# First expert layer of a two-layer transformer on one Trainium2 core: every expert on every row, or rows routed to their two experts

## The chip, the cores and the metric

The kernel runs on one core of one Trainium2 chip, in one launch. The metric is the device time in microseconds (us), the median of several executions. Engines are named as the profile names them: PE is TensorE, ACT ScalarE, DVE VectorE, POOL GpSimd, SP SyncE (it only issues DMAs here).

## The reference

4096 rows (4 sequences of 1024) of 128 numbers pass through attention, a mixture of experts, a second attention and a second mixture of experts, each behind a layer norm and added to x. The change touches the first mixture of experts:

```python
shared = new_gelu(xf @ Wfc_s + bfc_s) @ Wproj_s + bproj_s        # 128 -> 512 -> 128
probs = softmax(xf @ Wr)                                         # 8 experts
topk_p, topk_i = top_k(probs, 2)
topk_p = topk_p / sum(topk_p)
gate = zeros((N, 8)).at[arange(N)[:, None], topk_i].add(topk_p)
for e in range(8):
    h = new_gelu(xf @ Wfc[e] + bfc[e]) @ Wproj[e] + bproj[e]
    routed = routed + h * gate[:, e:e + 1]
out = shared + routed
```

Each row has a gate other than zero for two experts of eight. The reference computes all eight and multiplies by the gates.

## The kernel before

x stays in SBUF for the whole kernel as 32 tiles of 128 rows; a supertile is 4 tiles, 512 rows. The kernel is written engine by engine: in each stage every engine has its own instruction stream, in the order in which it is written, and waits on semaphores. Nothing is scheduled by a program; buffer numbers (`n % 3`, `n % 4`) and the waits set who is how far ahead.

The stages around the change are:

- `project_0` (L246) and `attention` (L443): the first attention, to 630 us. `SP` loads operands one and two steps ahead (L612 to L621). `project_out` adds its result to x and takes the statistics of the layer norm.
- `route` (L930), called as `r0`: all engines build what the experts need. DVE normalises rows (L205), PE turns them and makes the logits (L981, L989), ACT keeps them and makes a rounded high part (L1013, L1014), POOL the low part, which is the rest (L1050). Products are made of high and low parts, three for each (high x high, low x high, high x low). Then DVE finds the two largest of eight for all 32 tiles at once (`max` L1086, `match_replace` L1098, a chain of operations on 128x256, L1083 to L1106), POOL and DVE make low parts of the weights (L1055, L1110), and the gates are turned and stored in DRAM by expert (L967).
- `Absorb` (L1298): two small products of the second attention's weights, in PE's free time in `route`.
- `moe_0` (L1119): for each of 8 supertiles the shared expert and all 8 experts, each in 4 chunks of 128 hidden columns: 288 chunks. A chunk is three products into `f_ps` (L1183 to L1185), two Gelus on ACT (L1241: one full, one rounded), their difference on DVE (L1285), and three products into `y_ps` (L1199 to L1201). DVE multiplies each expert's result by its gate, broadcast over partitions by a 1 MB DMA for every four experts (L1173), and sums (L1261, L1265). At the end of a supertile PE turns the sum (L1211) and DVE adds it to x (L1270).

```python
for n in range(NH):                       # PE, one supertile
    fc(g, n)
    if n >= LAG:
        project(g, n - LAG)
```

Then `ln_stats` (L174) and `project_1` (L1340) of the second layer start.

## Time and profile before

| what | us |
|---|---|
| median of 3 executions | 2256.61 (2253.68 to 2261.46) |
| the profiled execution, its own time | 2258.54 |
| its span, first to last instruction | 2256.8 |
| PE busy in the span | 2087.3 (92%) |
| DVE busy | 1532.8 (68%) |
| ACT busy | 1378.1 (61%) |
| POOL busy | 471.1 (21%) |

A span is what the profile can see; about 2 us lie around it. Busy time of an engine is the time in which an instruction of it is under way; a busy PE is not PE at its peak. The granted clock is given as a share of the full one: 1.00 is 2.4 GHz, 0.50 is 1.2 GHz.

### The profile page before, as it was taken

To read this page: it belongs to the slowest core of one execution; us is meant where nothing else is said; L and a number is where in the kernel's file an instruction comes from. 1 tells how busy PE (TensorE), PEld (TensorE's weight loads), DVE (VectorE), ACT (ScalarE), POOL (GpSimd) and SP (SyncE) were. 2 spreads that over 40 slices of the span, in tenths; PEclk is the share of its full clock that TensorE was granted. 3 is DMA by queue.
4 is the path that set the end of the run, shared out by engine and by line. 5 is a ranking of instruction groups with operands and counts; after the bars stand their busy time and mean duration, and the time that the engine had idled before them with its cause. 6 is when DMAs were issued, how large, how long until landed. Compare 5 with 4: busy or idle time off the path is not lost. (4 is left out here: it accounts for less than half of the span.)

```text
span 2256.8 us, 42960 instructions
## 1 busy us (share of the span) xinstructions
PE 2087.3 (92%) x10730; PEld 1348.0 (60%) x10732; DVE 1532.8 (68%) x6213; ACT 1378.1 (61%) x2516; POOL 471.1 (21%) x804
## 2 busy tenths in 40 slices
PE   4799999999976999999899999999999998399998
PEld 3455555555465888888644555555555558278886
DVE  5778777877456777777766666666666634577776
ACT  4266666666656999889744555555555565355554
POOL 3011111111121000000001111111111111266766
PEclk9699999999976999999998999999999998599999
DMA  7324334334132112112094565556555611264753
GB/s 216 94 39 57 54 48 54 51 47 57 18 108 41 38 44 51 38 38 48 17 360 122 125 133 120 112 123 133 121 112 122 133 25 60 54 150 111 148 117 60
DMA packets 98869, 202.90 MB, mean 90 GB/s; under 512 B 13632, under 2 KB 35392, under 8 KB 98240
## 3 DMA queue, kind: packets, MB, share of 16 engines
q1 hardware_dynamic: 96496, 195.44, 39.8%
q10 hardware_dynamic: 2256, 6.21, 0.9%
q14 instruction: 81, 0.66, 0.1%
q8 instruction: 36, 0.59, 0.1%
HBM read 169.47 MB, written 31.60 MB: 89 GB/s over the span
## 5 line engine op out<-in xcount | busy, mean ns | idle before, releaser
L728 ACT ACTIVATE a1work<-a1T 128x512 f32<-128x512 f32 x576 | 331.4, 597 | 295.7 <-PE a1T L830 295.2
L671 DVE CUSTOM_DVE_ANT_0 a1ms<-a1S,mask_q 128x128 bf16<-128x128 f32 (+1 forms) x758 | 387.8, 553 | 172.5 <-issue 168.0
L671 DVE CUSTOM_DVE_ANT_0 a0ms<-a0S,mask_q 128x384 bf16<-128x384 f32 (+2 forms) x752 | 379.9, 553 | 103.0 <-issue 95.2
L728 ACT ACTIVATE a0work<-a0T 128x512 f32<-128x512 f32 x576 | 329.8, 597 | 192.1 <-PE a0T L830 181.6
L809 PE MATMUL a1O<-a1work,a1v 128*33 128x512 f32 (+3 forms) x1536 | 304.7, 496 | 0.9 <-POOL a1work L639 0.9
L830 PE MATMUL a0T<-a0qT,a0kT 128*128 128x512 f32 (+3 forms) x768 | 265.8, 393 | 16.0 <-ACT a0work L728 6.3
L1285 DVE TENSOR_TENSOR m_hl<-m_h,m_hh 128x512 fp32r<-128x512 f32 x288 | 197.6, 690 | 116.5 <-ACT m_hh L1241 111.7
L830 PE MATMUL a1T<-a1qT,a1kT 97*128 97x512 f32 (+3 forms) x768 | 263.7, 391 | 1.2 <-DMA a1qT<-a1mr 1.2
L769 PE MATMUL a0S<-a0kS,a0qS 128*128 128x384 f32 (+2 forms) x752 | 230.7, 363 | 26.6 <-PEq L298 14.8
L830 PEld LDWEIGHTS a1T<-a1qT,a1kT 97*128 97x128 f32 x768 | 132.0, 190 | 201.1 <-ACT a1work L728 144.4
L830 PEld LDWEIGHTS a0T<-a0qT,a0kT 128*128 128x128 f32 x768 | 131.9, 189 | 169.2 <-ACT a0work L728 125.9
L769 PE MATMUL a1S<-a1kS,a1qS 96*128 96x128 f32 (+1 forms) x758 | 219.9, 351 | 2.5 <-DVE a1held L668 1.7
L1241 ACT ACTIVATE m_h<-m_f,m_bfc 128x512 f32<-128x512 f32 x288 | 198.3, 689 | 38.8 <-PE m_f L1185 6.5
L1653 POOL TENSOR_TENSOR m_h<-m_pr,m_gb 128x512 f32<-128x512 f32 x128 | 186.5, 1474 | 85.8 <-DVE m_pr L1677 80.4
L1241 ACT ACTIVATE m_hh<-m_f,m_bfc 128x512 fp32r<-128x512 f32 x288 | 196.7, 683 | 0.0
L1662 DVE TENSOR_TENSOR m_hl<-m_h,m_hh 128x512 fp32r<-128x512 f32 x136 | 122.0, 897 | 81.4 <-ACT m_hh L1611 81.2
L769 PEld LDWEIGHTS a0S<-a0kS,a0qS 128*128 128x128 f32 x752 | 140.5, 196 | 51.5 <-issue 19.3
L1611 ACT CAST m_hh<-m_h 128x512 fp32r<-128x512 f32 x136 | 84.6, 622 | 125.3 <-POOL m_h L1653 117.6
L635 POOL TENSOR_TENSOR a1held<-ident 128x1 f32<-128x1 f32 x160 | 30.9, 193 | 600.7 <-ACT a1work L728 600.7
L809 PE MATMUL a0O<-a0work,a0v 128*9 128x512 f32 (+3 forms) x1536 | 150.7, 488 | 0.0
L769 PEld LDWEIGHTS a1S<-a1kS,a1qS 96*128 96x128 f32 x758 | 139.0, 193 | 15.2 <-DVE a1held L668 4.1
L809 PEld LDWEIGHTS a1O<-a1work,a1v 128*33 128x33 f32 x1536 | 64.8, 110 | 108.5 <-issue 78.2
(247 smaller groups left out, 3594.0 us busy)
## 6 DMA issues: line engine op xcount, KB each, us to landing
m_gb<-scr_g SPq DMA_DIRECT2D x48, 1024.0 KB, 8.8
a1qT<-scr_q SPq DMA_DIRECT2D x93, 256.0 KB, 4.1
a1qS<-scr_q SPq DMA_DIRECT2D x90, 256.0 KB, 6.5
a1kT<-scr_k SPq DMA_DIRECT2D x93, 128.0 KB, 4.9
a1kS<-scr_k SPq DMA_DIRECT2D x90, 128.0 KB, 7.1
scr_q<-attn SPq DMA_DIRECT2D x20, 512.0 KB, 5.3
scr_q<-p_own SPq DMA_DIRECT2D x16, 512.0 KB, 4.2
a0qT<-scr_q SPq DMA_DIRECT2D x45, 128.0 KB
```

Source lines behind the costliest of these rows:

```text
L635: nc.gpsimd.tensor_tensor(held[:, BANKS + p:BANKS + p + 1], k.ident[:, 0:1], k.ident[:, 0:1], ALU.add).then_inc(masked, 1)
L671: nc.vector.tensor_tensor_reduce(masked_s[spare][:, 0:c1 - c0], buf[:, 0:c1 - c0], k.mask_q[:, SEQ - w + c0:SEQ - w + c1], 1.0, NEVER, ALU ...
L728: nc.scalar.activation(prob_of(g, p)[:, h, :], t_ps[slot % 2][:, :], ACT.Exp, scale=scale)\
L769: last = nc.tensor.matmul(buf[:, c0 - first:c1 - first], qS[gU[1]][0:SROWS, h, i * P:(i + 1) * P], kS[gU[1]][0:SROWS, KI(h), c0:c1], start ...
L809: last = nc.tensor.matmul(o_ps[h * CT:h * CT + VW, q0:q1], vst[g[1]][:, seg[0], KI(h), :], prob_of(g, p)[:, h, off:off + q1 - q0], start=o ...
L830: last = nc.tensor.matmul(t_ps[slot % 2][:, off:off + q1 - q0], kT[g[1]][0:TROWS, KI(h), j * P:(j + 1) * P], qT[g[1]][0:TROWS, h, q0:q1], ...
L1241: nc.scalar.activation(dst[:, :], f_ps[n % 3][:, :], ACT.Gelu_apprx_tanh, bias=bfc[:, n:n + 1])\
L1285: nc.vector.tensor_tensor(hl[n % HBUF][:, :], h[n % 2][:, :], hh[n % HBUF][:, :].bitcast(F32), ALU.subtract).then_inc(hl_ready, 1)
L1611: nc.scalar.copy(hh[ring(g, e)][:, :], h[two(g, e)][:, :]).then_inc(hh_ready, 1)
L1653: nc.gpsimd.tensor_tensor(h[two(g, e)][:, :], prod[two(g, e)][:, :], gate, ALU.mult).then_inc(h_ready, 1)
L1662: nc.vector.tensor_tensor(hl[ring(g, e)][:, :], h[two(g, e)][:, :], hh[ring(g, e)][:, :].bitcast(F32), ALU.subtract).then_inc(hl_ready, 1)
```

## The change

`moe_0` now routes. `route` keeps only its form for the second layer. The new `moe_0` does all of this in one stage:

- In the first attention SP writes 16 blocks of padding rows (zeros, gate 0, and an index beyond the end) over `slot_rows`, a DRAM table of 36864 rows of 130 words: nine regions of 4096 rows.
- The shared expert runs first, 8 supertiles x 4 chunks = 32 chunks, with the chunk as before. Beside it DVE does the routing by quarters of 8 tiles (`quarter`): for each row and each of its two experts a place in that expert's region (counts over rows come from two small products on PE). DVE calls `gap()` between routing operations to do the shared expert's subtraction of the next chunk.
- When a quarter has its places, POOL issues 16 indirect DMAs, each writing 128 rows (normalised row, gate, own index) to `slot_rows`: 64 in all.
- `table()` makes from the eight counts, for each of 23 tiles of 512 rows, the expert and the block in DRAM. 23 is enough for any routing (16 full ones and 7 broken ones).
- For each tile: SP reads the block number into a register and loads 512 rows; PE turns them; ACT and DVE make high and low parts; DVE reads the expert's number into a register and copies that expert's weights into a buffer (four copies of 128x512); 4 chunks as before; PE turns the result back; DVE multiplies it by the rows' gates; POOL issues 4 indirect DMAs of 128 rows to `pair_rows`, by the rows' own index (padding rows fall out): 92 in all.
- At the end SP loads both halves of `pair_rows` and DVE adds them to x and takes the statistics. The products of `Absorb` come behind the last chunk; its loads behind the last weight copy.

The core of the diff (names of semaphores and waits that only moved are left out):

```diff
+SLOT_TILES = 2 * TOK // ST + 7
+SLOTS = 9 * TOK
...
@@ project_0, POOL: two fills ahead of the ones-buffers, of which there are 4 (before 3)
+                nc.gpsimd.memset(pad[:, :, 0:D + 1], 0.0)
+                nc.gpsimd.memset(pad[:, :, D + 1:ROW].bitcast(U32), SKIPPED)
@@ attention, SP, in each of 16 steps, ahead of the small row DMAs
+                    if each_step is not None:
+                        each_step(sp, g)
@@ moe_0, DVE, one quarter of the routing (its beginning is the old chain on 8 tiles)
+                gaps()
+
+                dve.wait_ge(summed, q + 1)
+                signal(tt(counts[:, q + 1, :], counts[:, q, :], pre0[:, LEAD + QT - 1, :], ALU.add))
+                at["counts", q] = count[0]
+                link(tt(sl[:, :, :], inclusive, sums[q].unsqueeze(1).broadcast_to([P, QT, E]), ALU.add))
+                at["summed", q] = count[0]
+                link(tt(sl[:, :, :], sl[:, :, :], mask, ALU.mult))
+                gaps()
+                link(reduce(second[:, :], sl[:, :, :], AXX, ALU.max), reduce(both[:, :], sl[:, :, :], AXX, ALU.add))
+                link(tt(first[:, :], both[:, :], second[:, :], ALU.subtract))
+                for i, place in enumerate((first, second)):
+                    signal(ts(slot[i][:, tiles], place[:, :], 1.0, None, ALU.subtract))
+                    link(tt(hit[:, :, :], sl[:, :, :], wide(place[:, :]), ALU.is_equal))
+                    link(tt(hit[:, :, :], hit[:, :, :], gt[:, :, :], ALU.mult))
+                    link(reduce(stage[i][:, tiles, D], hit[:, :, :], AXX, ALU.add))
+                    at["placed", q, i] = count[0]
+                gaps()
+
@@ moe_0, DVE, the routed tiles
+            def expert_of(t):
+                return dve.value_load(expert[0:1, t:t + 1], min_val=1, max_val=E)
+
+            def copy_fc(t, e):
+                for w, to in zip(wf, wfc[t % 2]):
+                    nc.vector.tensor_copy(to, w[:, bass.ds(e - 1, 1), :].rearrange("p o n -> p (o n)")).then_inc(wf_copied, 1)
+                nc.vector.tensor_copy(bfcc[:, t % 2, :], bfc[:, bass.ds(e, 1), :].rearrange("p o n -> p (o n)")).then_inc(wf_copied, 1)
+
+            def copy_project(t, e):
+                for w, to in zip(wp, wpc[t % 2]):
+                    nc.vector.tensor_copy(to, w[:, bass.ds(e - 1, 1), :, :].rearrange("p o c d -> p (o c d)")).then_inc(wp_copied, 1)
+                nc.vector.tensor_copy(bpc[:, t % 4:t % 4 + 1], bp[:, bass.ds(e - 1, 1)]).then_inc(wp_copied, 1)
...
+            for n in range(NSHARED, NSHARED + NT * NCH + 7):
+                t, ch = divmod(n - NSHARED, NCH)
+                if t < NT:
+                    split(n)
+                if t + 1 < NT:
+                    if ch == 0:
+                        e = expert_of(t + 1)
+                        copy_fc(t + 1, e)
+                    if ch == 1:
+                        split_x(t + 1)
+                    if ch == 3:
+                        copy_project(t + 1, e)
+                if ch == 2 and 0 <= t - 2:
+                    weigh(t - 2)
@@ moe_0, SP
+            sp.wait_ge(chain, at["table"])
+            sp.wait_ge(sent, 16 * 2 * TILES)
+            for t in range(NT):
+                b = sp.value_load(block_no[0:1, t:t + 1], min_val=0, max_val=SLOTS // ST - 1)
...
+                sp.dma_start(xt[t % XBUF].rearrange("p i c -> p (i c)"), rows).then_inc(x_loaded[t % NSEM], 16)
@@ moe_0, POOL
+            pool.wait_ge(*padded)
+            for q in range(NQ):
+                for i in range(K):
+                    pool.wait_ge(chain, at["placed", q, i])
+                    for t in range(q * QT, (q + 1) * QT):
+                        nc.gpsimd.indirect_dma_start(slot_rows, bass.IndirectOffsetOnAxis(ap=slot[i][:, t:t + 1], axis=0),
+                                                     stage[i][:, t, :], None).then_inc(sent, 16)
+
+            for t in range(NT):
+                if t >= NSEM:
+
+                    pool.wait_ge(y_sent[t % NSEM], 16 * TPS * on_sem(t - NSEM))
+                pool.wait_ge(yo_ready, t + 1)
+                for i in range(TPS):
+                    nc.gpsimd.indirect_dma_start(
+                        pair_rows, bass.IndirectOffsetOnAxis(ap=xt[t % XBUF][:, i, D + 1:ROW].bitcast(U32), axis=0),
+                        yo[t % XBUF][:, i, :], None, bounds_check=2 * TOK - 1, oob_is_err=False).then_inc(y_sent[t % NSEM], 16)
@@ transformer
+            def pad_slots(sp, g):
+                rows = slot_rows[bass.ds(lin(g, STEP, 0), STEP), :].rearrange("(p a m) c -> p a (m c)", p=P, m=3)
+                sp.dma_start(rows, a_q[:, 0:3 * ROW].unsqueeze(1).broadcast_to([P, STEP // P // 3, 3 * ROW])).then_inc(padded, 16)
+            project_out(k, "o0", attn, w_o, 4, w_o_loaded, load_weights)
-                route(k, "r0", 8, 2, router[0], None, xh, xl, gate_rows0, parts, sources, absorb)
-            moe_0(k, a["bfc"], a["L0_ffn_bproj"], a["L0_ffn_bproj_s"], wf, wp, xh, xl, gate_rows0)
+            moe_0(k, c, router[0], a["bfc"], a["L0_ffn_bproj"], a["L0_ffn_bproj_s"], wf, wp, h, stage, slot_rows, pair_rows,
+                  (padded, 16 * 16), [a[n] for n in ("L1_attn_Wq", "L1_attn_Wk_up", "L1_attn_Wv_up", "L1_attn_Wout")], a_q, a_v)
```

How the order of instructions moves, at three places. First DVE in the expert stage: of the kernel before, one and a half experts of a supertile. `m_hl` is the difference of the two Gelus, `m_pr` the result times gate, `m_acc` the sum.

```order
1160 L1261 SCALAR_TENSOR_TENSOR m_pr<-m_y,m_bp,m_gb 128x512
1161 L1265 TENSOR_TENSOR m_acc<-m_acc,m_pr 128x512
1162 L1285 TENSOR_TENSOR m_hl<-m_h,m_hh 128x512 x4
1163 L1261 SCALAR_TENSOR_TENSOR m_pr<-m_y,m_bp,m_gb 128x512
1164 L1265 TENSOR_TENSOR m_acc<-m_acc,m_pr 128x512
```

and of the change, the first three quarters of one routed tile (here `m_xh` and `m_xl` are also the buffers of copied weights, `stage` the weighed rows):

```order
1376 L1400 TENSOR_LOAD m_expert
1377 L1400 ISA x2
1378 L1404 ISA
1379 L1404 COPY m_xh<-wf 128x512
1380 L1404 REGISTER_ALU
1381 L1404 COPY m_xh<-wf 128x512
1382 L1405 ISA
1383 L1405 COPY m_bfcc<-m_bfc 128x4
1384 L1269 TENSOR_TENSOR m_hl<-m_h,m_hh 128x512
1385 L1414 TENSOR_TENSOR m_xh<-m_xT,m_xh 128x512
1386 L1269 TENSOR_TENSOR m_hl<-m_h,m_hh 128x512
1387 L1421 TENSOR_TENSOR stage<-m_l,stage 128x4x128
```

Between the subtractions, which were in rows of four, there now stand the register read, the weight copies (two here, two more behind the next subtraction), the low part of x and the weighing.

Second, DVE beside the shared expert in the change: the middle of one quarter of the routing. `m_sl` are the places, `m_xl` here the low part of x.

```order
1162 L1327 RECIPROCAL m_sm<-m_sm 128x8
1163 L1328 TENSOR_TENSOR m_gt<-m_rep,m_sm 128x64
1164 L1269 TENSOR_TENSOR m_hl<-m_h,m_hh 128x512
1165 L1289 TENSOR_TENSOR m_xl<-m_xs,m_xh 128x512
1166 L1332 TENSOR_TENSOR m_counts<-m_counts,m_pre 128x8
1167 L1334 TENSOR_TENSOR m_sl<-m_pre,m_l 128x64
1168 L1336 TENSOR_TENSOR m_sl<-m_sl,m_ch 128x64
1169 L1269 TENSOR_TENSOR m_hl<-m_h,m_hh 128x512
1170 L1338 TENSOR_REDUCE m_s<-m_sl 128x8 x2
```

The shared expert's subtractions come one by one between the small operations of the routing, which before stood in a stage of their own.

Third, POOL in the change, from the low parts of the shared weights to the end of the stage:

```order
112 L1519 TENSOR_TENSOR m_wsf<-m_h,m_wsf 128x512
113 L1519 TENSOR_TENSOR m_wsp<-m_h,m_wsp 128x512
114 L1523 TENSOR_TENSOR m_xl<-m_xs,m_xh 128x512 x4
115 L1530 DMA scr_slots<-stage,m_slot 36864x130 x64
116 L1539 DMA scr_pairs<-stage 8192x128 x92
```

Before, POOL had nothing in the expert stage; now it issues 156 indirect DMAs there.

## Rows read from the trace of the kernel before

**Rows 1.** The page: busy us of each engine, share of the span, instructions.

```profile
PE 2087.3 (92%) x10730; PEld 1348.0 (60%) x10732; DVE 1532.8 (68%) x6213; ACT 1378.1 (61%) x2516; POOL 471.1 (21%) x804
```

**Rows 2.** Windows by stage: length; busy time (instructions) by engine; clock, DMA share, GB/s.

```profile
0.00:630.00 630.00, 563.33 (x3391) 314.69 (x3393) 456.04 (x2518) 375.05 (x710) 110.98 (x225) 0.96 0.38 66
653.60:706.20 52.60, 31.69 (x168) 28.72 (x169) 33.32 (x142) 21.90 (x40) 21.80 (x14) 0.50 0.36 118
706.20:1115.60 409.40, 405.85 (x1760) 329.04 (x1760) 296.42 (x464) 363.06 (x577) 0.00 (x0) 0.99 0.20 42
```

**Rows 3.** Timeline of PE: start us, duration us. A chunk, the next, four transposes.

```profile
885.55 0.40 PE L1183 MATMUL m_f<-xh,wf 128*128 x1
...
886.94 0.40 PE L1183 MATMUL m_f<-xh,wf 128*128 x1
...
1113.34 0.66 PE L1211 MATMUL m_t<-ident,m_acc 128*128 128x128 f32 x4 [1.80 <-DVE m_acc L1265]
```

**Rows 4.** Timeline: two Gelus, an ACT copy, two DVE operations, none waiting.

```profile
709.80 0.68 ACT L1241 ACTIVATE m_hh<-m_f,m_bfc 128x512 fp32r<-128x512 f32 x1
710.37 0.69 ACT L1241 ACTIVATE m_h<-m_f,m_bfc 128x512 f32<-128x512 f32 x1
...
660.34 0.59 ACT L1013 COPY r0xs<-r0xT 128x512 f32<-128x512 f32 x1 [0.76 <-PE r0xT L981]
...
770.61 0.69 DVE L1285 TENSOR_TENSOR m_hl<-m_h,m_hh 128x512 fp32r<-128x512 f32 x1
771.22 0.68 DVE L1270 TENSOR_TENSOR x<-m_t,x 128x512 f32<-128x512 f32 x1
```

**Rows 5.** Timeline: first normalised rows, a table load, the next layer's statistics.

```profile
654.15 2.25 DVE L205 TENSOR_SCALAR r0xn<-x,mean,rstd 128x128 f32<-128x128 f32 x8 [0.54 <-PEq L174]
...
707.92 1.28 ACT L1241 ACT_TABLE_LOAD   x1 [4.58 <-PE m_f L1185]
...
1115.94 0.21 DVE L154 TENSOR_TENSOR mean<-stats 128x32 f32<-128x32 f32 x1 [0.31 <-PEq L1160]
```

**Rows 6.** Timeline of DVE: small operations.

```profile
652.41 0.19 DVE L162 SCALAR_TENSOR_TENSOR rstd<-dev,rstd 128x32 f32<-128x32 f32 x1
...
676.14 0.42 DVE L1083 TENSOR_REDUCE r0sm<-r0lg 128x32 f32<-128x256 f32 x1 [7.10 <-ACT r0lg L1018]
```

**Rows 7.** Groups of lines, 653.6 to 706.2: busy us, mean ns; DVE's small work.

```profile
L1098 DVE MATCH_REPLACE8 r0rep<-r0top,r0pr 128x14 f32<-128x14 f32 x32 | 4.6, 159 | 0.0
...
L1086 DVE MAX8 r0srt<-r0pr 128x8 f32<-128x8 f32 x32 | 2.3, 150 | 1.8 <-ACT r0pr L1028 1.8
```

**Rows 8.** POOL: an affine select (timeline) and the low part of x (groups).

```profile
2.15 0.29 POOL L316 TENSOR_SCALAR_AFFINE_SELECT ident<-ident 128x128 f32<-128x128 f32 x1 [0.23 <-POOL mask_q L314]
...
L1050 POOL TENSOR_TENSOR xl<-r0xs,xh 128x512 f32 x6 | 7.6, 1275 | 6.9 <-ACT xh L1014 6.9
```

**Rows 9.** Windows in the first projection, columns as in rows 2.

```profile
20.00:30.00 10.00, 9.89 (x55) 6.83 (x53) 9.19 (x16) 7.24 (x14) 8.11 (x3) 1.00 0.90 317
40.00:50.00 10.00, 5.07 (x24) 3.02 (x22) 2.10 (x4) 1.96 (x4) 0.00 (x0) 0.97 0.72 210
```

**Rows 10.** Timeline 680 to 692: POOL's subtractions and DVE beside and behind them.

```profile
680.25 10.22 POOL L1055 TENSOR_TENSOR wf<-wf_raw,wf 128x1536 fp32r<-128x1536 f32 x3 [5.11 <-ACT wf L1032]
...
681.16 2.63 DVE L1087 TENSOR_TENSOR r0top<-r0srt 128x64 f32<-128x64 f32 x1
...
688.49 2.26 DVE L1100 TENSOR_TENSOR r0rep<-r0rep,r0pr 128x256 f32<-128x256 f32 x1
690.79 0.43 DVE L1101 TENSOR_TENSOR r0rep<-r0rep,r0pr 128x256 f32<-128x256 f32 x1
```

**Rows 11.** DMA issues: KB each, median us from issue to landing.

```profile
x<-L_attn_x SPq DMA_DIRECT2D x4, 512.0 KB, 6.0
...
out<-x SPq DMA_DIRECT2D x8, 256.0 KB, 2.4
...
scr_g<-r1gs SPq DMA_DIRECT2D x32, 8.0 KB, 1.4
```

More of the change, by code:

```diff
@@ L1762, in transformer @@
                 rest, stores, v_stores = project_0(k, a["L0_attn_x"], a["L0_attn_q_heads"], a["L0_attn_k_heads"], a["L0_attn_v_heads"],
                                                    load_more, q0, k0, v0, rows, ring, v_rows,
-                                                   [work[:, 6144 + n * D:6144 + (n + 1) * D] for n in range(3)])
-                attention(k, "a0", 4, 8, 8.0 ** -0.5, rows, attn, work, rest, wait_stored(stores + v_stores), stores[0:2] + v_stores)
-            project_out(k, "o0", attn, w_o, 4, w_o_loaded)
@@ new lines, in transformer @@
+                attention(k, "a0", 4, 8, 8.0 ** -0.5, rows, attn, work, rest, wait_stored(stores + v_stores), stores[0:2] + v_stores,
+                          pad_slots)
+            wf = [sb(c, f"wf{i}", [P, 8, 512], F32R) for i in range(2)]
+            wp = [sb(c, f"wp{i}", [P, 8, 4, D], F32R) for i in range(2)]
+            h = [sb(c, f"m0_h{i}", [P, ST]) for i in range(2)]
+            parts = [(h[0][:, :], a["Wfc"][:, 0]), (h[1][:, :].rearrange("p (c d) -> p c d", d=D), a["Wproj"][:, 0])]
```

806 lines of the change are left out of this document (557 added, 249 removed).

## The prediction

> **What bounds the kernel now.** I read the busy shares first, then the windows by stage, then the groups of lines in the expert stage, and last the timeline inside it. TensorE is busy 92% of the span [rows 1]. The change touches two stages: the router (653.6 to 706.2) and the first expert layer (706.2 to 1115.6) [rows 2]. In the expert stage TensorE is busy 405.9 of 409.4 us at clock 0.99: it is the bound there. One chunk (three products into the hidden layer, three out) starts every 1.39 us: 885.55, then 886.94 [rows 3], so a product takes 0.231 us, and 288 chunks make 400 us. ScalarE's two Gelus and VectorE's subtraction of 0.69 us each per chunk lie beside that. When they are not waiting, Gelus start every 0.57 us and VectorE operations on 128x512 every 0.61; a ScalarE copy is 0.59 long [rows 4]. The router is the contrary: a chain through all engines at half clock (0.50) [rows 2], and its TensorE work is small. From the first normalised row at 654.15 to the next layer's statistics at 1115.94 less a gap of 0.3 [rows 5] it is 461.5 us. This stretch is what the change replaces.
>
> **The sum.** Chunks fall from 288 to 32 shared plus 23 x 4 = 124, so the products fall from 400 to 172 us. The 228 us aren't all won, for three reasons: other engines become the bound, routing adds a chain, and rows must travel through DRAM.
>
> *First stretch: normalise, route, scatter, beside the shared expert.* VectorE has the most work here. A quarter of the routing has 24 linked small operations on 8 to 64 elements. Such operations last 0.19 us at 32 elements and 0.42 at 256 [rows 6]; I take 0.26 from start to start, so 6.2 us. Eight normalised rows at 2.25/8 are 2.25 [rows 5], eight MAX8 at 2.28/32 are 0.6, eight replacements at 4.6/32 are 1.2 [rows 7], the shift 0.3. That is 10.5 a quarter, 42 in all. To it come 32 subtractions, 8 additions to x and 4 low parts of x (44 x 0.61 = 27), 32 rows for the logits (9), 16 low parts of weights (16 x 0.61 = 10) and the table (14 operations, 4). Sum 92 us of VectorE, against 32 x 1.39 = 44 of TensorE. What VectorE can't fill: the first chain from normalise to exponentials (about 10, since GpSimd's 1.28 us low parts [rows 8] and a 1.28 us table load [rows 5] stand in it), bursts of five subtractions in a row that outrun TensorE (2 for each of three quarters, 6), and the clock. The clock was 0.97 in a window with 5.1 of 10 us busy [rows 9], but 0.50 (1.2 of 2.4 GHz) throughout the router [rows 2]; here TensorE will be busy about half of the time. I add 6 (none to 20). ScalarE reloads its table twice for each of three more exponentials, 7.7 us, beside 32 pairs of Gelus (36): it is not the bound here. Total 114: the first routed tile starts near 768. Are the scattered rows there? The last places are known about 30 us earlier (near 738), and 16 of 64 indirect DMAs follow them. Nothing in this trace shows what such a DMA costs GpSimd. The nearest rows are its small instruction (0.29, an affine select) and its subtraction of 128x512 (1.28) [rows 8]; the far end is its longest, 3.4 us (three in 10.22) [rows 10]. A DMA with 128 separate addresses is nearer to the operation on all columns: I take 1.3. Then 16 x 1.3 = 21, landing 2 (8 KB land in 1.4 us, 256 KB in 2.4 [rows 11]), reload 3: 764 to 767, just hidden. The Trainium skill (DMA: Bandwidth & Descriptors, "Anatomy of one DMA") puts about 2.0 us fixed on such a DMA, mostly the write receipt, and calls generation small; by that the issue would be shorter than 1.3 and the whole sum some 8 us less. No row here shows it.
>
> *Routed stretch: 23 tiles.* TensorE: 24 products at 0.231 are 5.54; two sets of four transposes, 0.66 where they stand alone [rows 3], make 6.9 at most; among products they overlap, so 6.6. ScalarE: 8 x 0.57 + 2 x 0.59 = 5.7. VectorE: four subtractions, one low part, one weighing (6 x 0.61 = 3.7); four copies of 128x512 from SBUF to SBUF; two tiny copies 0.2; the read of the expert's number into a register, plus the wait for ScalarE's copy of x in the same slot. The copy is bounded by 0.28 (a quarter of the columns, [rows 5]) and 0.68 (an operation that reads PSUM, [rows 4]); I take 0.45, so 1.8. The read is not in the trace; between nothing and the 1.4 us of the smallest landing [rows 11] I take 0.7. VectorE 6.4 in all. GpSimd: 4 x 1.3 = 5.2. Three engines within 1 us of each other, tied by buffers two and three deep, don't overlap fully: I take 7.4 (6.6 to 9.5), 23 x 7.4 = 170. SP's loads are four to eight tiles ahead; hidden.
>
> *Tail.* Last tile through projection, transpose and weighing 3.5; its four scatters 5.2; landing 2; then the second half of the pair rows, four quarters of 512 KB. 2.1 MB at the 317 GB/s of a busy window [rows 9] are 6.6, the first quarter's latency between the 2.4 and the 6.0 of a 256 and a 512 KB load [rows 11]: 9.6 together. Last addition of 1024 columns and eight statistics, 3. Together 23. The small products of the second attention's weights come behind the last chunk and lie beside scatter and reload.
>
> *Elsewhere.* GpSimd's two fills and a fourth ones-buffer at the start: 1 us at most. The padding writes 19.2 MB in 16 DMAs inside the first attention, whose DMA share is 0.38 at 66 GB/s [rows 2]: 30 GB/s more fits, they are issued ahead of the small row DMAs, not behind their waits. From nothing to 4 us a step (1.2 MB at 317 GB/s [rows 9]); I take 0, as loads run one or two steps ahead. If that cover is gone it is 64 us, a rival below. The removed 32 stores of gate rows and 16 broadcasts of 1 MB free DMA nobody waited for after 706.
>
> New 114 + 170 + 23 = 307 against 461.5: 154.5 saved, 1 added elsewhere. The profiled execution took 2258.5 (span 2256.8), 1.9 above the median of 2256.6. So 2258.5 - 153.5 = 2105.0 there, **2103 as a median**.
>
> **Rivals.**
> 1. *Full overlap.* The tile costs TensorE's 6.6 and the first stretch loses nothing to clock and bursts: -18, -12, tail -6: **2067**. For it: before, TensorE ran within 1% of its products. Against: there VectorE was idle almost a third of the time [rows 2]. Chance 0.15.
> 2. *VectorE and GpSimd hold each other up.* Beside GpSimd's long subtractions, a VectorE operation on 64 elements took 2.63 us and one on 256 took 2.26, while the next of that size took 0.43 [rows 10]. If each pair of weight copies meets an indirect DMA, it loses 1.05 us on each: 7.4 + 2.1 = 9.5 a tile, +48: **2151**. For it: GpSimd would be at work 5.2 of 7.4 us. Against: filling in addresses may not hold what a subtraction holds. Chance 0.20. The Trainium skill (SBUF - State Buffer, "Who interferes with whom") says that a VectorE copy from SBUF to SBUF and GpSimd's descriptor writing take the same exclusive port pair, whoever starts first; that speaks against this change, and the case's rows agree for two-input operations only [rows 10].
> 3. *GpSimd's issue is the bound: slower.* At c us an indirect DMA the first stretch ends at 674 + 64c + 5 and a tile takes 4c once c passes 1.85. The excess over the forecast is (64c - 89) + (92c - 170) = 156c - 259, which eats the 154.5 at **c = 2.65**. At the far end, 3.4, it is +271: **2374**. For it: 156 such DMAs, none measured. Against: 3.4 us belongs to 1536 columns. Chance 0.06 beyond 2.65; another 0.05 between 1.85 and 2.6 (2133 to 2250).
> 4. *The padding isn't hidden.* Attention's PE waits for its loads (16 steps x 4 us): +64, **2167**. The kernel then pays in a stage that the change should leave alone. Chance 0.05. That it does not do what it says (say, more than 23 tiles) is excluded by the count, which is fixed in the program.
>
> **Numbers.** Forecast 0.49, rivals 0.15, 0.20, 0.11, 0.05. The range 2066 to 2172 takes in 1, 2 and 4; what is left out is the upper part of 3 and the tails. A difference of 0.3% (7 us) is about what can be told from none: faster 0.93, same 0.01, slower 0.06.
>
> **What would show it.** First routed product at 768 (755 to 790); start to start of a tile 7.4; VectorE the busiest engine before it; mean of a weight copy 0.45 (over 1 us: rival 2); GpSimd's indirect DMA 1.3 (over 2: rival 3) with idle time between them in the routed stretch; last scatter's landing to next layer's statistics about 13; attention's end still near 630 (later: rival 4). The forecast is wrong in kind if TensorE waits in the routed stretch for loads of rows or for the scatter.

## The result, and the profile after

The changed kernel takes **2145.5 us** (2140.4 to 2150.0, 4 runs) against 2256.9 (2253.7 to 2261.5, 4 runs): ratio 0.9515, 95% interval 0.9497 to 0.9533. It saves 111 us; the forecast was 2103 (2066 to 2172), a saving of 154. The sign and the range held; 42 us of the saving did not come, and the range held in part because terms that were too small and one that was too large offset each other (below). The profiled execution took 2149.99 us (span 2148.3), 45.0 more than the 2105.0 of the sum.

The first milestones are in the page (busy us by engine, then PE's granted clock in 40 slices), which answers to [rows 1]:

```profile
span 2148.3 us, 40438 instructions
PE 1909.2 (89%) x9931; PEld 1194.0 (56%) x9933; DVE 1436.7 (67%) x6262; ACT 1205.2 (56%) x2247; POOL 628.3 (29%) x972
PEclk9699999999996778996889999999999996799999
```

Then the replaced stretch by windows, columns as in [rows 2]: up to the first quarter's places, three quarters, from the last places to the first routed product, the 23 tiles to the last product into the hidden layer, and the tail to the next layer's statistics.

```profile
668.90:690.00 21.10, 16.21 (x62) 13.46 (x62) 17.26 (x76) 11.90 (x18) 10.28 (x23) 0.54 0.01 1
690.00:719.20 29.20, 13.63 (x54) 10.65 (x54) 15.12 (x71) 12.69 (x22) 15.95 (x16) 0.71 0.12 38
719.20:750.50 31.30, 19.47 (x89) 15.34 (x89) 18.16 (x78) 20.46 (x34) 16.05 (x16) 0.78 0.11 35
750.50:780.50 30.00, 17.68 (x63) 13.28 (x64) 15.56 (x69) 17.46 (x28) 15.47 (x16) 0.72 0.11 36
780.50:816.50 36.00, 19.61 (x71) 14.50 (x70) 24.21 (x53) 11.19 (x18) 15.37 (x16) 0.74 0.30 90
816.50:965.30 148.80, 147.59 (x713) 119.95 (x714) 122.81 (x265) 133.72 (x225) 90.59 (x79) 0.98 0.20 58
965.30:1002.50 37.20, 13.95 (x85) 10.82 (x83) 20.32 (x47) 2.54 (x4) 13.09 (x13) 0.59 0.60 142
```

Three things are to be seen. In the tiles TensorE is busy 147.6 of 148.8 us, at clock 0.98: it is the bound there, as it was before. In the three quarters **no engine is near full**: VectorE, the busiest by the forecast, works 15 to 18 of 30 us. And the tail is 37 us. Set against the terms of the sum:

| part | forecast | measured | difference |
|---|---|---|---|
| first normalised row, against 654.15 [rows 5] | +1 | 668.90: +14.75 | +13.8 |
| first stretch, to the first routed product (816.53) | 114 | 147.6 | +33.6 |
| 23 tiles, to the last product into the hidden layer (965.3) | 170 | 148.8 | -21.2 |
| tail, to the next statistics (1002.82) | 23 | 37.5 | +14.5 |
| from there to the end of the span (1140.9 before) | 1140.9 | 1145.5 | +4.6 |

The sum is +45.3. So four terms were too small and one too large, and each has to be found by itself.

**Where the stage starts 14.8 us later.** The first attention, from the first `a0S` to the last `a0O`, took 569.0 us before and takes 587.8 (57.2 to 645.0; it begins 2.7 us earlier, so the next stage starts less late than that). The view of one line, L680 (a memset that opens each of VectorE's units there, L668 before), tells what ended the idle time of the engine ahead of it:

```profile
L680 DVE MEMSET a0held<- x768: 59/59/59, 58.0 to 611.5; 128x1 f32 x192
  issue: 20.5, 5
  PE a0S L781: 2.5, 7
  PE a0S L781: 19.8, 7
```

The fourth row counts who waited for it: TensorE, 19.8 us. Before, the same line had no idle time under "issue" (10.0 us under TensorE), and TensorE waited for it 6.2 us. Five stalls of 3.6 to 4.5 us in which VectorE waits for nothing that the profile shows stand at 227.8, 300.2, 372.6, 444.4 and 516.2: every 72 us, which is two steps, one pass of the loop body. Here is one: SP's padding DMA (first row), VectorE (second), then all DMA between 292 and 302 us (GB/s in 40 slices, the queue that brings instructions with its packets, MB and share, and the padding's KB and us to landing):

```profile
293.26 0.63 SPq L2195 DMA_DIRECT2D scr_slots<-a_q  x1
300.22 0.06 DVE L680 MEMSET a0held<- 128x1 f32 x1 [4.18 <-issue]
GB/s 0 0 0 0 0 0 16 0 0 0 287 374 374 387 399 362 368 362 368 287 312 331 275 193 127 19 0 0 0 0 0 0 0 0 33 0 0 0 0 0
q14 instruction: 2, 0.02, 0.5%
scr_slots<-a_q SPq DMA_DIRECT2D x1, 1170.0 KB, 6.4
```

The padding fills the DMA engines for about 4 us, lands at 299.7, and VectorE goes on at 300.2. Two packets of instructions came in these 10 us, one in each of the microseconds from 298 and from 300. That is theory A: VectorE branches back, must fetch its loop's first instructions by DMA, and the fetch is held up by the padding. The trace's own records of branches and packets bear it out (they do not say which engine a packet is for): after VectorE's branch of each of the five stalled passes the first packet starts 2.7 to 3.9 us later, and VectorE goes on 2.2 to 2.6 us behind that packet. In the kernel before it is 1.0 to 1.3 and 1.9 to 2.2. So each pass has a fetch in either kernel; beside the padding it comes 1.4 to 2.9 us later. The Trainium skill (Runtime: NRT & Kernel Launch, "Instruction fetch mechanics") says that a taken branch out of the window that is held forces a DMA fetch before execution goes on; by that the place of the stall is what the trace shows. That section says nothing of other transfers ahead of the fetch.

**Where the quarters lose their time.** VectorE's linked small operations of the second quarter (L1316 to L1321), GpSimd's indirect DMAs and ScalarE's Gelu beside them:

```profile
701.43 0.23 DVE L1316 TENSOR_TENSOR m_ch<-m_rep,m_pr 128x64 bf16<-128x64 f32 x1
702.85 0.19 DVE L1321 TENSOR_TENSOR m_pre<-m_ch 128x64 bf16<-128x64 bf16 x1 [1.19 <-DVE m_ch L1316]
703.56 0.19 DVE L1321 TENSOR_TENSOR m_pre<-m_pre 128x64 bf16<-128x64 bf16 x1 [0.52 <-DVE m_pre L1321]
704.96 0.19 DVE L1321 TENSOR_TENSOR m_pre<-m_pre 128x64 bf16<-128x64 bf16 x1 [1.21 <-DVE m_pre L1321]
704.20 0.96 POOL L1530 DMA_INDIRECT scr_slots<-stage,m_slot  x1 [0.30 <-issue]
707.10 0.69 ACT L1720 ACTIVATE m_h<-m_f,m_bfc 128x512 f32<-128x512 f32 x1 [4.66 <-remote]
712.91 0.59 ACT L1704 COPY m_xs<-m_xT 128x512 f32<-128x512 f32 x1 [4.54 <-remote]
716.37 0.16 DVE L1332 TENSOR_TENSOR m_counts<-m_counts,m_pre 128x8 bf16<-128x8 bf16 x1 [7.29 <-PE m_l L1570]
```

An operation of 0.19 us starts 0.5 to 1.2 us after the one it depends on has ended, though both are VectorE's own. ScalarE waits 4.66 us, "remote": a semaphore rose just then, but no instruction that raises it had just ended. The trace also records each rise of a semaphore. The Gelu at 707.10 waited for TensorE's product; that product ended at 701.8, and its increment is recorded at 707.08. The copy at 712.91 waited for transposes that ended at 703.8; their increment came at 712.89. So **the work was done and its semaphore came late**. I measured this for all instructions: from the end of one to the next recorded rise of its semaphore (rises that come together are recorded as one). The median and the ninth decile, in us:

```
                               PE            DVE           ACT
before, from 706 us on         0.01 0.02     0.01 0.01     0.01 0.01
change, 64 scatters (690-801)  2.61 9.24     0.01 2.32     0.01 6.06
change, tiles (837-965)        0.01 3.67     0.01 6.45     0.01 2.55
```

These distances are no bound in either direction: a rise that has no record of its own counts up to the next one. In the tiles that is most of it (the large values are one tile, 6.45 us, or multiples of it, and some pass 1000 us), although TensorE is busy 99% there. The safe count is of waits that ended at a recorded rise over 0.3 us after the end of every instruction that could have raised it. Among the 64 scatters it finds 18 waits of VectorE for its own operations (13.6 us, at most 1.21 late) and 6 of ScalarE for TensorE (15.4 us, at most 9.11 late); in the tiles 5 of ScalarE, 1.7 us; in the kernel before, from 706 to 1115, none.

That is theory B: while GpSimd issues indirect DMAs, increments of other engines arrive late. A wait shows it for TensorE's and VectorE's; for ScalarE's only the table does. VectorE's wait for its count (7.3, 4.2 and 3.8 us in the three quarters) is where it comes together, since TensorE's count stands in program order behind products that wait for ScalarE.

### The profile page after: what moved, and what is told of

It is laid out like the page before. It is cut to its first block and busy times, and to the rows that moved or that the text cites. A ratio compares the mean times of both kernels' runs of the same rounds, so it can differ in the third digit from the quotient of the medians.

```text
span 2148.3 us, 40438 instructions
## 1 busy us (share of the span) xinstructions
PE 1909.2 (89%) x9931; PEld 1194.0 (56%) x9933; DVE 1436.7 (67%) x6262; ACT 1205.2 (56%) x2247; POOL 628.3 (29%) x972
## 5 line engine op out<-in xcount | busy, mean ns | idle before, releaser
L781 PE MATMUL a0S<-a0kS,a0qS 128*128 128x384 f32 (+2 forms) x752 | 233.8, 368 | 36.9 <-DVE a0held L680 19.8
L2095 DVE TENSOR_TENSOR m_hl<-m_h,m_hh 128x512 fp32r<-128x512 f32 x136 | 122.2, 898 | 83.0 <-ACT m_hh L2044 82.9
L647 POOL TENSOR_TENSOR a0held<-ident 128x1 f32<-128x1 f32 x80 | 15.6, 195 | 520.6 <-ACT a0work L740 520.6
L1539 POOL DMA_INDIRECT scr_pairs<-stage x92 | 103.7, 1127 | 78.4 <-DVE stage L1421 46.2
L1269 DVE TENSOR_TENSOR m_hl<-m_h,m_hh 128x512 fp32r<-128x512 f32 x124 | 85.9, 693 | 42.5 <-ACT m_hh L1720 25.8
```

The costliest lines, as they stand in the source:

```text
L647: nc.gpsimd.tensor_tensor(held[:, BANKS + p:BANKS + p + 1], k.ident[:, 0:1], k.ident[:, 0:1], ALU.add).then_inc(masked, 1)
L781: last = nc.tensor.matmul(buf[:, c0 - first:c1 - first], qS[gU[1]][0:SROWS, h, i * P:(i + 1) * P], kS[gU[1]][0:SROWS, KI(h), c0:c1], start ...
L1269: tt(hl[n % HBUF][:, :], h[n % 2][:, :], hh[n % HBUF][:, :].bitcast(F32), ALU.subtract).then_inc(hl_ready, 1)
L1539: nc.gpsimd.indirect_dma_start(pair_rows, bass.IndirectOffsetOnAxis(ap=xt[t % XBUF][:, i, D + 1:ROW].bitcast(U32), axis=0), yo[t % XBUF][: ...
L2095: nc.vector.tensor_tensor(hl[ring(g, e)][:, :], h[two(g, e)][:, :], hh[ring(g, e)][:, :].bitcast(F32), ALU.subtract).then_inc(hl_ready, 1)
```

## The experiments

Experiments 1 to 4 ran on one chip, 5 to 7 on a second, 8 to 11 on a third and 12 on a fourth, each group with the kernel before beside it. Experiments 2, 3, 4, 7, 10 and 11 are one execution each, the others four or five. The edits are shown as excerpts. "Attention" is the span from the first `a0S` to the last `a0O`; "quarters" are the distances from the last places of one quarter to those of the next (29.9, 31.3, 30.0 us in the change).

**1. Padding in every second step.** `pad_slots` returns where `g[1]` is 1 and takes twice the rows otherwise:

```diff
-            STEP = SLOTS // 16
+            STEP = SLOTS // 8
+                if g[1]:
+                    return
```

> The same 19.2 MB of padding, but in 8 DMAs of 2.4 MB, issued in the first step of each pair of steps of the first attention; none is issued where the engines' loops branch back (the loop body holds two steps). Theory A (an instruction fetch of VectorE queued behind the padding at the branch): the five gaps of 3.6 to 4.5 us before L680 with no releaser are gone, the first attention (first a0S to last a0O) falls from 587.8 to 569-573 us (569.0 before the change), the total from 2145.5 to 2126-2132. Rival A' (the padding's 19.2 MB slow the operand loads, or share memory with them): the volume is the same, so the attention stays at 584-592 and the total at 2141-2150.

Measured: 2092.2 us (2089.4 to 2094.8), ratio to before 0.9281 (0.9266 to 0.9297). Attention 566.2, below the range given; on the same chip it is 583.5 and 579.3 in experiments 3 and 4, whose padding is that of the change. The same view of L680:

```profile
L680 DVE MEMSET a0held<- x768: 59/59/59, 53.6 to 585.5; 128x1 f32 x192
  PE a0S L781: 9.5, 12
  PE a0S L781: 6.7, 9
```

No "issue" is left, although the same 19.2 MB are written in DMAs twice as large, landing in 12.1 us instead of 6.7. The first packet starts 1.0 to 1.3 us after each of VectorE's five branches again. The volume is hidden; its place at the branch was not. Theory A holds, A' falls. But the total fell by 53, not by 15 to 20, and the rest is in a stretch that the edit does not touch:

```profile
644.20:665.30 21.10, 16.20 (x62) 13.45 (x62) 17.26 (x76) 11.90 (x18) 10.21 (x24) 0.53 0.01 1
665.30:686.10 20.80, 14.41 (x61) 11.37 (x62) 15.68 (x74) 12.99 (x22) 15.99 (x16) 0.75 0.16 50
686.10:712.00 25.90, 18.83 (x87) 14.90 (x87) 17.50 (x75) 19.93 (x33) 16.40 (x17) 0.87 0.14 45
712.00:734.10 22.10, 16.08 (x66) 11.95 (x65) 15.49 (x69) 17.45 (x28) 15.45 (x16) 0.85 0.15 49
734.10:763.80 29.70, 15.66 (x62) 10.81 (x60) 23.80 (x53) 11.14 (x18) 17.33 (x16) 0.81 0.22 66
763.80:910.90 147.10, 147.06 (x713) 120.68 (x714) 124.14 (x265) 134.84 (x226) 94.38 (x79) 0.98 0.23 67
910.90:948.40 37.50, 12.66 (x84) 10.74 (x82) 20.28 (x47) 2.53 (x4) 13.07 (x13) 0.58 0.59 140
```

The same work (VectorE 15.7, 17.5, 15.5 us) in windows of 20.8, 25.9 and 22.1 us; quarters 20.8, 26.6, 22.1. The first stretch is 119.7, near the 114 of the sum. No increment of TensorE is more than 0.03 us late here in the scatters.

**2. Padding behind the attention.** The 16 DMAs go to `load_weights`, behind the weights.

```diff
+                for g in range(16):
+                    pad_slots(sp, g)
```

> The padding leaves the attention altogether: SP issues the same 16 DMAs behind the loads of the expert weights, while the attention's output is projected. Theory A and rival A' both say that the first attention falls to 569-572 us; if it stays above 580, neither is right and another part of the change (start of the program, the SP queue's order) costs it. After it: 19.2 MB at about 317 GB/s are 60 us from 640 on, so GpSimd's first scatter moves from 22 us after the first normalised row to 30-45, and the last scatter with it unless the quarters catch up.

Measured: 2153.3 us; attention 564.3, which falls as both said, to 5 us below their range. SP was held until 692 us by issuing them (the statistics behind `project_out` stand at 692.7, its last product at 638.3), so the whole stage starts late: first scatter at 723.7, 28.4 us after the first normalised row (30 to 45 expected). Between those two it is 54.4 us, against 3.7 in the change: padding at the wrong time costs 51 us, near the 64 of rival 4, at another place. Increments were not late here either; quarters 20.8, 25.5, 21.6.

**3. Scatters only after the last quarter.**

```diff
-                    pool.wait_ge(chain, at["placed", q, i])
+                    pool.wait_ge(chain, at["placed", NQ - 1, K - 1])
```

> GpSimd issues none of the 64 scatters before the last quarter's places are known. Theory B (while GpSimd issues indirect DMAs, the engines' semaphore increments arrive late): without them the quarters' places follow each other by 18-22 us instead of 29-31, linked operations of VectorE stand 0.2-0.3 us apart everywhere, and no engine waits for a semaphore of work long done. Rival B' (in-order waits of TensorE and ScalarE for each other, ScalarE's table loads, the half clock): the distance stays at 27-31 us. The 64 scatters then take 64 x 1.27 = 81 us at the end: last one issued 81 us after the last places; by theory B the total is 2160-2180, by the rival 2195-2210.

Measured: 2172.4 us; places 20.7, 26.6 and 22.1 apart, last scatter 81.3 us after the last places. Distances and total are those of theory B, but they tell nothing: the two kernels before it, with scatters in place, have the same distances to 1.1 us. On this chip no engine waited for a late increment beside indirect DMAs. What it gives is that, where increments are not late, VectorE loses nothing to GpSimd's issue: 20.7, 26.6, 22.1 without, 20.8, 26.6, 22.1 with.

**4. The rows sent by SP.** 64 plain DMAs of the same rows, issued by SP at the same points.

```diff
+                    sp.wait_ge(chain, at["placed", q, i])
+                    for t in range(q * QT, (q + 1) * QT):
+                        r = (i * TILES + t) * P
+                        sp.dma_start(slot_rows[r:r + P, :], stage[i][:, t, :]).then_inc(sent, 16)
```

> The 64 scatters of 128 rows of 520 bytes become 64 plain DMAs of the same rows to consecutive rows of the same scratch, issued by SP at the same points (so rows reach no expert regions and the sums are other ones; the pair rows are filled beforehand). Theory B (it is GpSimd's writing of descriptors that delays the semaphores): quarters 18-22 us apart, as with late scatters. Rival B'' (it is the transfers of small rows with their 16 increments each, whoever issues them): 27-31 us apart, linked operations again 0.5-1.2 us late.

Measured: 2118.4 us, quarters 20.7, 25.6, 21.6. Inconclusive for the same reason. (The first quarter's places come 30.9 us after the first normalised row, against 19.4 in experiment 1; so they do, to 0.2 us, in experiments 10 and 11, which also fill the pair rows beforehand. Totals of these three carry that.)

**5. The change again, unedited.**

> The changed kernel, nothing edited, as a control: in its first profile semaphore increments arrive up to 9 us late (TensorE 8.9 us in the median of the first quarter's scatters, VectorE 0.8) while GpSimd issues indirect DMAs, but in the four kernels that followed they arrive within 0.01 us beside the same DMAs. Theory B1 (the delay belongs to the chip or moment of that first measurement): here the quarters' places stand 20-26 us apart, the first attention stays at 580-588 us, and the total is 2108-2120, some 30 below the first result. Theory B2 (the delay belongs to this kernel, and moving the padding took it away): quarters 29-31 us apart again, 2140-2150.

Measured: 2143.7 us (2141.6 to 2145.5), ratio 0.9501; attention 584.9, places 29.9, 31.3 and 30.0 apart, TensorE's increments 3.35 us late in the median, 17 waits of VectorE for itself and 6 of ScalarE for TensorE ended by late rises (12.3 and 15.7 us). The two theories do not yet part here, as neither kernel nor chip is that of experiment 1.

**6. Padding in every second step, count ahead.** On TensorE:

```diff
+                if n in COUNT_AT:
+                    count(COUNT_AT[n])
                 if 0 <= n - LAG < NSHARED:
                     project(n - LAG)
-                if n in COUNT_AT:
-                    count(COUNT_AT[n])
```

> Padding every second step as in the kernel that took 2092, and on TensorE the count of a quarter's rows (two small products for which VectorE waits) stands ahead of the chunk's second three products, which wait for ScalarE's copy of y. Theory C (TensorE's fixed order is what VectorE waits for at the count, 2.8 + 3.5 + 2.6 = 8.9 us in that kernel): the wait falls to 0-2 us, places follow each other by 18-22 us, total 2084-2088. Rival C' (VectorE only waits elsewhere, for ScalarE's Gelus): the wait moves to L1269, total 2090-2094.

Measured, beside experiment 5: 2118.1 us (2113.5 to 2123.3), 25.6 below it; attention 568.0; TensorE's increments late again (4.05 in the median), with the padding moved. That refutes B2: the delay stays when the padding goes, and what differs from experiments 1 to 4 is the chip, or the moment. The totals expected for C and C' were for a chip without delays, so this run decides nothing between them. Quarters are 26.5, 30.8 and 29.3.

**7. No rows sent back.** The 92 indirect DMAs of the tiles and the waits for them are left out.

> Leaves out the 92 indirect DMAs that send weighed rows back (so the pair rows hold other rows, filled beforehand); everything else as in the change. Theory D (TensorE is the bound in the routed stretch: 24 x 0.231 + 8 transposes = 6.2-6.4): start to start of a tile stays at 6.3-6.5 us. Rival D' (GpSimd's 4 x 1.27-1.58 = 5.1-6.3 us a tile and its hold on VectorE set the pitch): it falls to 6.0 or below. Tail: GpSimd's backlog of 12 us between last weighing and last indirect DMA falls away, last product to the next layer's statistics 37 -> 22-26 us.

Measured: 2134.0 us, on the chip of 5 and 6. In the first stretch, with its scatters, TensorE's increments are 4.72 us late in the median; in the tiles, where none is issued and SP still loads rows, the largest is 0.02 on every engine. One execution holds both, so what GpSimd issues matters, not the chip alone. The tiles take 146.7 us: TensorE sets them (theory D). Experiment 5 has 150.9, but experiment 6, on the same chip and with the rows sent back, has 146.6, and 8 to 11 have 146.2 to 146.6; a price of the indirect DMAs in the tiles is not shown. From the last weighing to the next statistics it is 22.0 us against 33.1, from the last hidden product 26.8 (22 to 26 expected). The copies of weights for the next tile, in experiment 5 (first row: shortest, median, longest ns) and here:

```profile
L1404 DVE CAST m_xh<-wf x46: 417/427/711, 806.4 to 951.4; 128x512 fp32r x46
```

```profile
L1404 DVE CAST m_xh<-wf x46: 416/424/429, 810.0 to 950.7; 128x512 fp32r x46
```

Some copies take up to 0.3 us more beside indirect DMAs: a hold such as rival 2's exists, at less than a tenth of its price (the mean of this pair is 498 against 423 ns; that of the other pair, L1409, 423 against 420). The Trainium skill (SBUF - State Buffer, "Who interferes with whom") says that such a copy and GpSimd's descriptor writing share a port pair, and that TensorE and ScalarE wait for nobody there; by that rule TensorE's late increments, up to 9.2 us among the scatters of experiments 5 and 7, are another thing than this hold.

**8 and 9. Padding alone, and padding with the count, side by side.** The kernels of experiments 1 and 6.

> The first experiment's kernel again (padding in every second step), beside the next one on one chip. So far semaphore increments came late beside GpSimd's indirect DMAs in the measurement of the change and in all three kernels of the second job, in none of the four of the first. Theory B1 (a matter of the chip): where this chip shows the delay, this kernel takes 2118-2128; where not, 2090-2095.

> The kernel with the count ahead of the second products again, now beside the one without. Theory C (VectorE waits for the count because of TensorE's order): 3-7 us faster than its neighbour on either kind of chip, places of the second to fourth quarter 2-4 us closer together. Rival C': within 2 us of it.

Measured: 2119.7 us (2117.0 to 2122.6), ratio 0.9398 (0.9382 to 0.9414), and 2111.8 (2110.6 to 2116.6), ratio 0.9366 (0.9350 to 0.9381). Experiment 8 is the very kernel that took 2092.2 with ratio 0.9281 on the chip of experiment 1: the intervals are far apart, and B1 holds (no run parts the chip from the moment). Its first stretch takes 145.5 us instead of 119.7, its tiles and tail 184.0 against 184.8, so the whole difference is in the first stretch. The count ahead gives 7.9 us: places 26.4, 28.8, 27.0 apart instead of 29.7, 31.0, 29.8. C holds, slightly over its range; the first stretch alone is 7.8 us shorter. VectorE's waits in both, longest first:

```profile
DVE m_counts L1332 <- PE m_l L1570: 18.4, 3, 8.4
DVE m_hl L1269 <- ACT m_hh L1720: 13.1, 6, 5.5
```

```profile
DVE m_hl L1269 <- ACT m_hh L1720: 11.1, 6, 3.6
DVE m_counts L1332 <- remote: 9.0, 2, 4.6
```

The wait for TensorE's order is gone; what is left of the wait for the count is a late increment ("remote").

**10. The rows sent by SP, on a chip that delays.** Experiment 4's edit on the kernel of experiment 9.

> Padding and count as in its neighbour; the 64 scatters of the first stretch are plain DMAs of the same rows issued by SP to consecutive rows (the sums are other ones; the pair rows are filled beforehand), while the 92 indirect DMAs that send rows back in the routed stretch stay with GpSimd, as a control inside the kernel. If this chip shows the delay (late increments in the routed stretch): theory B (indirect DMAs issued by GpSimd cause it) says no increment over 0.1 us late in the first stretch and quarters 20-23 us apart; rival B'' (the transfers of small rows themselves) says late there too, 27-31 us apart. If it does not show the delay, 20-26 us in both.

Measured: 2099.2 us. This is the experiment that 4 should have been, because it has two controls. Its neighbour, experiment 9, on the same chip: among its scatters VectorE waited 12 times for itself (8.2 us), ScalarE 6 times for TensorE (14.9 us) and VectorE twice for TensorE (8.8 us), each ended by a late rise. Here, among the 64 plain DMAs, there is no such wait, and the distance to the next rise is at most 0.03 us. And its own routed stretch, with GpSimd's indirect DMAs: ninth deciles of 6.45, 6.46 and 1.74 us, which are for the most part rises without a record (never seen in experiment 1's tiles), and two late rises that ScalarE waited for, 0.7 us. Quarters 18.7, 24.5, 19.9 (20 to 23 expected), against 26.4, 28.8, 27.0. The same operations as above:

```profile
692.86 0.22 DVE L1316 TENSOR_TENSOR m_ch<-m_rep,m_pr 128x64 bf16<-128x64 f32 x1
693.12 0.19 DVE L1321 TENSOR_TENSOR m_pre<-m_ch 128x64 bf16<-128x64 bf16 x1
693.34 0.42 DVE L1321 TENSOR_TENSOR m_pre<-m_pre 128x64 bf16<-128x64 bf16 x2
```

The steps are 0.22 to 0.26 us again. Theory B holds, B'' falls: the same small rows sent by SP delay nothing, sent by GpSimd's indirect DMAs they do. That the rows go to consecutive places here was not varied by itself, nor were plain DMAs issued by GpSimd.

**11. Half of the rows in each scatter**, on the kernel of experiment 9.

```diff
-  bass.IndirectOffsetOnAxis(ap=slot[i][:, t:t + 1], axis=0), stage[i][:, t, :], None)
+  bass.IndirectOffsetOnAxis(ap=slot[i][0:64, t:t + 1], axis=0), stage[i][0:64, t, :], None)
```

> As its neighbour, but each of the 64 scatters takes 64 of the 128 rows (the other half of the rows is left out; the pair rows are filled beforehand): as many DMAs and as many increments, half of the descriptors and bytes. Theory B3 (the delay grows with the descriptors): on a chip that shows it, GpSimd's 0.96 us fall to about 0.6, and the quarters are 23-26 us apart instead of 27-31, with a smaller median delay of TensorE's increments. Rival B4 (it is the number of DMAs and of their increments): 27-31 us apart as with whole scatters, or worse, since they follow each other faster.

Measured: 2131.5 us; 0.91 us a DMA against 1.00, quarters 27.2, 37.3, 27.1, TensorE's increments 3.20 late in the median (2.71 in experiment 9). Halving the rows relieves nothing; why the second distance grew to 37.3 is not known. B3 falls; that it is the number of DMAs (B4) fits, but no run issued fewer of them, so this stays open.

**12. Weighed earlier.** The tail: the last three weighings in experiment 9, then GpSimd's first DMA behind them and its last.

```profile
927.78 0.68 DVE L1421 TENSOR_TENSOR stage<-m_yT,stage 128x512 f32<-128x512 f32 x1
929.86 0.69 DVE L1421 TENSOR_TENSOR stage<-m_l,stage 128x512 f32<-128x512 f32 x1 [0.60 <-issue]
931.99 0.69 DVE L1421 TENSOR_TENSOR stage<-m_yT,stage 128x512 f32<-128x512 f32 x1 [1.44 <-PE m_yT L1644]
929.30 0.98 POOL L1539 DMA_INDIRECT scr_pairs<-stage  x1 [0.58 <-issue]
943.47 0.98 POOL L1539 DMA_INDIRECT scr_pairs<-stage  x1 [0.30 <-issue]
```

Twelve DMAs of 1.29 us from start to start stand in one row, where the forecast had the last tile's four. The edit: `keep_y` in chunk 2 of the next tile instead of 3, `turn_y` in chunk 0 instead of 1, `weigh` in chunk 0 instead of 2.

> Padding every second step and count ahead, as in the kernel that took 2111.8, and in the routed stretch a tile's y is copied, turned and weighed one to two chunks earlier. Before, the weighings of the last three tiles stand 2.1 us apart (927.8, 929.9, 932.0), so that 12 indirect DMAs of 1.29 us queue on GpSimd behind the last product; the last one starts 11.5 us after the last weighing. Theory E (that queue is the tail's excess over the prediction): with earlier weighing the last indirect DMA starts 6-10 us after the last weighing, last weighing to the next layer's statistics falls from 32.7 to 27-31 us, tiles stay at 6.0-6.1 us, and the total is 2106-2111 on a chip that delays increments, 2080-2087 on one that does not. Rival E' (TensorE or ScalarE then waits for y in each tile): the tile grows to 6.2-6.5 us and eats it, 2110-2120.

Measured: **2087.4 us** (2080.9 to 2092.1, 5 runs), ratio 0.9255 (0.9227 to 0.9282), on a chip that does not delay. The last three weighings stand at 909.00, 913.39 and 915.97, the last indirect DMA starts 9.0 us after the last (11.5 before), last weighing to statistics is 30.3 (32.7), the tiles take 146.7, that is 6.38 each as in experiment 9 (6.36) and not the 6.0 to 6.1 expected. Experiment 6 shows 8.8 and 30.3 without this edit, so the firmer sign is the whole tail from the last hidden product, 35.2 us against 37.4 to 37.9 in the runs above that send the rows back, save 38.4 in experiment 11. E's direction holds, and the gain is small. The total is 0.4 us above its range, within the spread. It is 4.8 us less than in experiment 1 on another such chip, for count and weighing together, but the intervals of the two ratios overlap, so that total is not clear of noise.

VectorE's wait for the count is 2.2 us here (8.9 in experiment 1), and the last places are known 7.6 us sooner after the first scatter, yet the first stretch is only 1.2 us shorter (118.5 against 119.7). GpSimd's scatters say why (count, then busy us and mean ns, then idle us before them), in experiment 1 and here:

```profile
L1530 POOL DMA_INDIRECT scr_slots<-stage,m_slot x64 | 65.2, 1018 | 33.3 <-issue 17.1 <-DVE stage L1344 8.1 <-DVE m_slot L1341 6.9
L1530 POOL DMA_INDIRECT scr_slots<-stage,m_slot x64 | 70.5, 1101 | 27.0 <-issue 18.6 <-DVE stage L1344 7.8 <-DVE m_ends L1360 0.3
```

Its waits for places (6.9 us) are gone; from its first scatter at 667.1 to the end of the last at 756.8 it is never idle for over 0.5 us, and the scatters themselves have become 5.3 us longer in all. With the count ahead and no late increments, GpSimd's issue is what bounds this stretch.

## Why the prediction was right, and where its steps failed

The large terms held. The chunks fell from 288 to 124 at TensorE's pace, sign and range came right, the indirect DMA (forecast 1.3, far end 3.4) takes 0.98 us in the mean in the first stretch and 1.13 in the tiles, with 0.30 more before the next (so 1.28 to 1.29 from start to start in an undisturbed row), and rival 3 was never near its 2.65. Padding apart, the sum's 307 us for the replaced stretch is 304.5 in experiment 1. That closeness is luck: 119.7, 147.0 and 37.8 stand there against 114, 170 and 23. Against the measurement the steps did this:

- *"The padding ...: I take 0, as loads run one or two steps ahead."* This step failed: +13.8 us. The loads did run ahead; TensorE waited for none of them over 1 us, but for one of 3.1 at the start (3.9 before). What was behind the padding was a transfer that no line of the kernel issues, VectorE's fetch of its own loop. Experiments 1 and 2 show it: 566.2 and 564.3, against 587.8 in the change and 583.5 and 579.3 with the same padding on their own chip.
- *"Sum 92 us of VectorE ... Total 114."* VectorE's work was as counted, 90.3 us in the first five rows above. The first stretch took 147.6 on a chip that delays increments, 119.7 on one that does not. The missing term, 26 to 28 us, is the late semaphores; in the sum a linked operation had 0.26 us from start to start, and beside scatters it had 0.7 to 1.4. Nothing in the profile of before could show it, since GpSimd issues no DMA there. What the clock cost of its 6 us is not separated: the granted clock is 0.54 to 0.78 over the first stretch of the change and 0.53 to 0.87 over that of experiment 1. The sum also gave nothing for TensorE's order (8.9 us of waiting for the count even without delays; 6.7 of that wait goes in experiment 12, though not of the stretch). And the end was not VectorE's: *"landing 2 ..., reload 3: 764 to 767, just hidden"* was the path itself. From the end of the last scatter to the first routed product it took 7.8 us in experiment 1 instead of 5, and 16.0 in the change, where ScalarE first waited 7.3 us for TensorE, 5.3 of them behind the end of the product.
- *"I take 7.4 ..., 23 x 7.4 = 170."* Too high by 21: 6.47 a tile, and 6.36 to 6.39 in the experiments save the fifth (6.56). Three engines within 1 us of each other did overlap; TensorE, busy 99%, set the pace, and its eight transposes added 0.8 to 0.9 us to the products' 5.54. This error hid a third of the others: 21 of 66 us.
- *The tail, "Together 23"* (3.5 + 5.2 + 2 + 9.6 + 3). It measured 37.5. In experiment 9's trace: last weighing done 5.5 after the last hidden product, twelve scatters instead of four (11.8 instead of 5.2), landing 4.2 instead of 2, the first quarter of the reload 4.2, and then VectorE, 11.6 for four additions and 32 statistics where I had 3 after the last reload. The mechanism was there, its sizes too small, and the queue of twelve missed.
- *Elsewhere.* From the next statistics to the end it is 1145.5 instead of 1140.9, and 1142.6 to 1146.4 in the experiments. About 3.5 us are one wait: GpSimd's first operation in the second expert layer waits 8.5 us for broadcast gate rows from DRAM instead of 5.0. Why that load lands later wasn't tried.

Of the rivals, 4 named the right stage, with a mechanism (loads) that did not happen; 2 had the right suspicion, that GpSimd's issue slows others, and the wrong path; the copies measured 0.42 to 0.50 us where it needed over 1. 3's price is nowhere near, but its mechanism is what bounds the first stretch in experiment 12. The experiments' best kernel, 2087.4, is faster than both the kernel before and the change.

## What to carry to other kernels

When bulk DMA is added "where bandwidth is free", look where the engines' loops branch back: in these traces instructions come by DMA too, after each branch, and they are in no list of loads. An issue moved by one step, with twice the size, cost nothing here. And where an engine waits and its releaser ended long ago, compare the recorded rise of the semaphore with the end of the instruction before blaming an engine's order, and count only rises that an engine is seen to wait for, since some have no record; then repeat the same kernel on another chip before explaining a difference. A control inside the same execution, as the two stretches of experiment 7 were, or on the same chip, as experiment 9 was for 10, is worth more than one on another.

## What was not expected of the hardware

- While GpSimd issued indirect DMAs, engines waited for increments of TensorE that came up to 9 us late (12.8 in experiment 11) and of VectorE up to 3.6 (experiment 7): on the chip of experiments 5 to 7, on that of 8 to 11, and in the first measurement, and not on those of 1 to 4 and of 12. None was late beside SP's DMAs of the same rows (0.03 us at most). The kernel before, which issues no indirect DMA, took 2256.1, 2256.1 and 2256.9 us on the first three and 2252.6 and 2252.1 on the other two. What sets the chips, or the moments, apart is not known.
- Where a DMA of 1.17 MB was under way at its loop's branch, VectorE stood idle 3.6 to 4.5 us for its instructions; without it 1.3 to 1.6.
- An indirect DMA of 64 rows costs GpSimd 0.91 us and one of 128 rows 0.96 to 1.00: almost nothing depends on the rows.
